# Last normalisation moved to ScalarE, limit copies moved to ScalarE, similarities ahead of the up projection

## What is computed

```python
q = jnp.einsum('bnd,de->bne', x, w_q)
q = (q - mean) * jax.lax.rsqrt(var + BN_EPS) * bn_gamma + bn_beta
sim = jnp.einsum('pbnhd,hkpd->pbnhk', q, keys)
sx, ix = jax.lax.top_k(sim[0], TOPK)
sy, iy = jax.lax.top_k(sim[1], TOPK)
all_scores = (sx[..., :, None] + sy[..., None, :]).reshape(b, n, H, TOPK * TOPK)
scores, pk = jax.lax.top_k(all_scores, TOPK)
h = jnp.einsum('bnd,bnhkd->bnhk', x, wd)
h = jax.nn.softmax(scores, axis=-1) * gelu_new(h)
out = jnp.einsum('bnhk,bnhkd->bnd', h, wu)
...
x = _layernorm(x + out)
```

## Time and profile before

| | us |
|---|---|
| median of 3 runs | 690.45 |
| lowest, highest | 686.77, 692.17 |
| the profiled execution, whole | 690.42 |
| its span | 688.1 |
| busy in the span: PE, DVE, ACT, POOL | 536.6, 559.7, 356.8, 442.5 |

### The profile page before, as it was taken

How to read it: one execution, slowest core, us unless ns; L and a number is a source line. 1 busy time by engine, 2 the same in 40 slices (tenths; PEclk the granted TensorE clock), 3 DMA queues, 4 the chain that set the end, 5 groups by cost and what they waited for, 6 DMA issues and landing times.

```text
span 688.1 us, 42215 instructions
## 1 busy us (share of the span) xinstructions
PE 536.6 (78%) x17863; PEld 455.5 (66%) x17863; DVE 559.7 (81%) x1837; ACT 356.8 (52%) x557; POOL 442.5 (64%) x615
## 2 busy tenths in 40 slices
PE   0475999999996899965667868778778778778765
PEld 0364888888885676855366757667667667667655
DVE  6544799899895678865698989999999999999962
ACT  4334577777774477751435445455445445445350
POOL 7533465655642344442387887898888898888870
PEclk9978899999999999986589999999999999999996
DMA  6786575654534010000032231322332331331320
GB/s 215 221 265 185 151 235 167 215 173 156 179 97 170 16 32 17 16 1 8 9 71 54 68 72 46 70 69 53 69 72 50 72 72 46 75 70 46 71 65 19
DMA packets 44934, 64.60 MB, mean 94 GB/s; under 512 B 5456, under 2 KB 37072, under 8 KB 42320
## 3 DMA queue, kind: packets, MB, share of 16 engines
q1 hardware_dynamic: 44880, 63.84, 33.1%
HBM read 36.29 MB, written 8.65 MB: 65 GB/s over the span
## 4 chain that ended last, share of the span: by engine, by line
PE 47%; DVE 31%; issue 14%; POOL 4%; ACT 1%; DMA 1%; DVEq 1%; SPq 0%; POOLq 0%; ACTq 0%
PE ps L743 9%; DVE top L1339 6%; PE ps L931 6%; PE ps L758 5%; PE ps L723 5%; PE ps L804 5%; DVE prod L1394 4%; PE ps L817 4%; DVE wq_sb L1370 4%; PE ps L733 3%; PE ps L910 3%; DVE best L1350 3%; DVE r_x L1379 3%; DVE hid L1385 2%; PE ps L769 2%
## 5 line engine op out<-in xcount | busy, mean ns | idle before, releaser
L931 PE MATMUL ps<-up_sb,prod 128*128 128x128 f32 x512 | 80.8, 320 | 48.5 <-DVE prod L1394 47.9
L931 PEld LDWEIGHTS ps<-up_sb,prod 128*128 128x128 f32 x512 | 74.4, 228 | 54.9 <-DVE prod L1394 54.4
L952 ACT ACTIVATE arena<-ps 128x512 f32<-128x512 f32 x128 | 70.2, 595 | 63.0 <-PE ps L743 62.9
L910 PE MATMUL ps<-arena,hid 128*32 128x32 f32 x8192 | 82.0, 200 | 23.9 <-issue 20.1
L910 PEld LDWEIGHTS ps<-arena,hid 128*32 128x32 f32 x8192 | 77.0, 112 | 29.3 <-issue 21.5
L658 POOL TENSOR_TENSOR wq_sb<-wq_sb,tile_rows 128x1024 f32<-128x1024 f32 x32 | 76.2, 2380 | 8.4 <-POOL tile_rows L654 7.2
L1072 ACT ACTIVATE out_tile<-ps,shift,rstd 128x128 f32<-128x128 f32 x32 | 14.6, 457 | 123.5 <-POOL shift L682 123.5
L1126 DVE TENSOR_REDUCE row_max<-ps 128x8 f32<-128x768 f32 x64 | 61.0, 952 | 19.8 <-PE ps L733 19.8
L743 PE MATMUL ps<-ident,arena 128*128 128x128 f32 x512 | 72.3, 288 | 1.1 <-issue 1.1
L919 PEld LDWEIGHTS ps<-xT,downT_sb 128*128 128x128 f32 x512 | 64.6, 198 | 11.9 <-issue 11.0
L1129 DVE TENSOR_TENSOR arena<-ps,row_max 128x768 f32<-128x768 f32 x64 | 61.3, 957 | 5.1 <-DVE row_max L1126 0.2
(11 more groups left out here) (157 smaller groups left out, 1299.0 us busy)
## 6 DMA issues: line engine op xcount, KB each, us to landing
arena<-r_x SPq DMA_DIRECT2D x128, 128.0 KB, 2.4
early<-terms SPq DMA_DIRECT2D x8, 720.0 KB
xT<-terms SPq DMA_DIRECT2D x8, 720.0 KB
hid<-terms SPq DMA_DIRECT2D x8, 720.0 KB
prod<-terms SPq DMA_DIRECT2D x8, 720.0 KB
x_pair<-in_x_wrapped SPq DMA_DIRECT2D x16, 256.0 KB, 2.6
x<-in_x SPq DMA_DIRECT2D x8, 256.0 KB, 2.8
xT_tile<-xT SPq DMA_DIRECT2D x32, 64.0 KB, 1.9
```

The source lines that it names most:

```text
L910: mm = nc.tensor.matmul(slots[32 * g:32 * g + 32, k, c], leftT[p][:, r // 2, r % 2, :], blocks_of[p][:, :, r // 2, r % 2, GROUP * g:GROUP ...
L931: mm = nc.tensor.matmul(ps[:, 6 + p, 0:P], pairs[:, c // 2, c % 2], up_sb[:, c, :], start=False, stop=(c == EC - 1))
L952: return nc.scalar.activation(out_ap, in_ap, ACT.Copy)
```

## The change

Four parts. (1) The last normalisation: DVE's bn_stats, bn_aggr and addition go; ACT takes minus the mean by a scaled Copy with an accumulated output (last_mean), the sum of squares by Square with the bias minus the mean (last_square), the variance plus epsilon (last_variance), and after POOL's power also the shift. POOL keeps the power alone (last_power), now of tile t - 3 and between the scaling of the exponentials and that of the right masks. (2) The two copies of limits go from POOL to ACT (set_limits); POOL's next tops and its thresholds wait for limits_set. (3) On PE the similarities of tile t + 2 stand ahead of the up projection of tile t - 1. (4) rel_exp is laid out with the eight heads of a key side by side: ACT writes with a step of 8 elements, POOL reads with a step of 1.

```diff
...
         limits = two("limits", [P, PK_HEADS, 10])
-        rel_exp = [tile_rows[:, 2560 + 512 * p:3072 + 512 * p].rearrange("p (a k) -> p a k", a=PH) for p in range(2)]
+        rel_exp = [tile_rows[:, 2560 + 512 * p:3072 + 512 * p].rearrange("p (a k h) -> p a k h", a=2, h=PK_HEADS) for p in range(2)]
...
                 pool.wait_ge(top_done, t + 1)
+                need(pool, limits_set, t)
                 hold(pool)
...
                 xs, ys = top_rel[:, 0:PK_HEADS, :], top_rel[:, PK_HEADS:PH, :]
-                nc.gpsimd.tensor_copy(limits[p][:, :, 2:5:2].rearrange("p h a -> p a h"),
-                                      top_rel[:, :, 1].rearrange("p (a h) -> p a h", a=2))
-                nc.gpsimd.tensor_copy(limits[p][:, :, 7:10:2], stretch(top_rel[:, 0:PK_HEADS, 1:2], 2))
                 nc.gpsimd.tensor_tensor(cand[:, :, 0:16].rearrange("p h (a b) -> p h a b", a=2),
...
                 pool.wait_ge(best_done, t + 1)
+                pool.wait_ge(limits_set, t + 1)
                 hold(pool)
...
-            def scale_right(t, p):
+            def scale_exps(t, p):
...
                 hold(pool)
-                ey = rel_exp[p][:, PK_HEADS:PH, :]
-                nc.gpsimd.tensor_tensor(ey, ey, bcast(rz[p][:], 2, KEYS), ALU.mult).then_inc(scaled, 1)
+                ey = rel_exp[p][:, 1]
+                nc.gpsimd.tensor_tensor(ey, ey, bcast(rz[p][:], 1, KEYS), ALU.mult).then_inc(scaled, 1)
+            def scale_right(t, p):
                 pool.wait_ge(scaled, t + 1)
...
                 hold(pool)
-                nc.gpsimd.tensor_tensor(right[p], right[p], bcast(ey.rearrange("p h j -> p j h"), 3, TERMS), ALU.mult
+                nc.gpsimd.tensor_tensor(right[p], right[p], bcast(rel_exp[p][:, 1], 3, TERMS), ALU.mult
                                         ).then_inc(right_ready, 1)
...
                 hold(pool)
-                ex = rel_exp[p][:, 0:PK_HEADS, :].rearrange("p h i -> p i h")
+                ex = rel_exp[p][:, 0]
                 nc.gpsimd.tensor_tensor(left[p][:, :, :, 0:TERMS - 1], left[p][:, :, :, 0:TERMS - 1],
...
-            def last_scale(t):
-
+            def last_power(t):
                 pool.wait_ge(d_var, t + 1)
-                hold(pool)
-                nc.gpsimd.tensor_tensor(rstd4[:], var4[:], minus_half[:, 0:1], ALU.pow).then_inc(rstd_step, 1)
-                pool.wait_ge(rstd_step, t + 1)
-                hold(pool)
-                nc.gpsimd.tensor_scalar(shift4[:], mom4[:, 0:1], rstd4[:], -1.0, ALU.mult, ALU.mult).then_inc(d_rstd, 1)
+                need(pool, out_ready, t)
+                hold(pool)
+                nc.gpsimd.tensor_tensor(rstd4[:], var4[:], minus_half[:, 0:1], ALU.pow).then_inc(d_rstd, 1)
...
                     t, o = 2 * i + p, 1 - p
+                    if have(t):
+                        scale_exps(t, p)
+                    if have(t - 3):
+                        last_power(t - 3)
                     if have(t):
...
                         scale_left(t, p)
-                    if have(t - 2):
-                        last_scale(t - 2)
             over_tiles(pool, d_pool)
+            last_power(NT - 1)
...
                     t, o = 2 * i + p, 1 - p
+                    if have(t + 2):
+                        similarities(t + 2, p, i + 1)
                     if have(t - 1):
                         up_projection(t - 1, o)
-                    if have(t + 2):
-                        similarities(t + 2, p, i + 1)
                     if have(t + 1):
...
                 need(a, left_ready, t - 1)
-                nc.scalar.activation(rel_exp[p].rearrange("p a k -> p (a k)"), ps[:, p, :], ACT.Exp
+                nc.scalar.activation(rel_exp[p].rearrange("p a k h -> p a h k"),
+                                     ps[:, p, :].rearrange("p (a h k) -> p a h k", a=2, h=PK_HEADS), ACT.Exp
                                      ).then_inc(relexp_done, 1)
+            def set_limits(t, p):
+                a.wait_ge(top_step, t + 1)
+                need(a, masked, 2 * (t - 1))
+                copy(limits[p][:, :, 2:5:2].rearrange("p h a -> p a h"), top_rel[:, :, 1].rearrange("p (a h) -> p a h", a=2))
+                copy(limits[p][:, :, 7:10:2], stretch(top_rel[:, 0:PK_HEADS, 1:2], 2)).then_inc(limits_set, 1)
+            def last_mean(t, p):
+                a.wait_ge(up_done, t + 1)
+                nc.scalar.activation(scratch[:], ps[:, 6 + p, 0:P], ACT.Copy, scale=-1.0 / P, accum_out=minus_mean4[:]
+                                     ).then_inc(d_mean, 1)
+            def last_square(t, p):
+                a.wait_ge(d_mean, t + 1)
+                nc.scalar.activation(scratch[:], ps[:, 6 + p, 0:P], ACT.Square, bias=minus_mean4[:], accum_out=square4[:]
+                                     ).then_inc(d_square, 1)
+            def last_variance(t):
+                a.wait_ge(d_square, t + 1)
+                nc.scalar.activation(var4[:], square4[:], ACT.Identity, bias=eps_col[:], scale=1.0 / P).then_inc(d_var, 1)
             def last_norm(t, p, i):
                 a.wait_ge(d_rstd, t + 1)
+                nc.scalar.activation(shift4[:], minus_mean4[:], ACT.Copy, scale=rstd4[:]).then_inc(d_shift, 1)
+                a.wait_ge(d_shift, t + 1)
                 need(a, stored[p], 16 * i)
...
+            a.wait_ge(eps_ready, 1)
             a.wait_ge(w_sim_done, 1)
...
                         rel_exps(t + 1, o)
+                        set_limits(t + 1, o)
+                    if have(t - 2):
+                        last_mean(t - 2, p)
+                    if have(t + 1):
                         best_exps(t + 1, o)
                     if have(t - 2):
+                        last_square(t - 2, p)
+                        last_variance(t - 2)
                         last_norm(t - 2, p, i - 1)
...
-            def last_moments(t, p):
-                v.wait_ge(up_done, t + 1)
-                V.bn_stats(stats4[:], ps[:, 6 + p, 0:P]).then_inc(d_step, 1)
-                v.wait_ge(d_step, 2 * t + 1)
-                need(v, out_ready, t)
-                hold(v)
-                V.bn_aggr(mom4[:], stats4[:]).then_inc(d_step, 1)
-                v.wait_ge(d_step, 2 * t + 2)
-                V.tensor_scalar(var4[:], mom4[:, 1:2], EPS, None, ALU.add).then_inc(d_var, 1)
-
             v.wait_ge(x3_kept, NQ)
...
                         top_keys(t + 1, o)
-                    if have(t - 2):
-                        last_moments(t - 2, p)
                     if have(t):
```

More of the change, by code:

```diff
@@ L216, in attention_and_product_keys @@
         out_tile = two("out_tile", [P, P])
-        stats4 = sb("stats4", [P, 6])
-        mom4 = sb("mom4", [P, 2])
+        scratch = sb("scratch", [P, P])
+        eps_col = sb("eps_col", [P, 1])
+        minus_mean4 = sb("minus_mean4", [P, 1])
+        square4 = sb("square4", [P, 1])
         var4 = sb("var4", [P, 1])
@@ L317, in attention_and_product_keys @@
         up_done = sem("up_done")
-        d_step = sem("d_step")
+        eps_ready = sem("eps_ready")
+        limits_set = sem("limits_set")
+        d_mean = sem("d_mean")
+        d_square = sem("d_square")
         d_var = sem("d_var")
-        rstd_step = sem("rstd_step")
         d_rstd = sem("d_rstd")
+        d_shift = sem("d_shift")
         out_ready = sem("out_ready")
@@ L496, in _ @@
             nc.gpsimd.memset(ones[:], 1.0)
+            nc.gpsimd.memset(eps_col[:], EPS).then_inc(eps_ready, 1)
             nc.gpsimd.memset(zeros[:], 0.0)
@@ L1311, in split_constants @@
                 cols = slice(Q_SPLIT[part].start * KEYS, Q_SPLIT[part].stop * KEYS)
-                c_rest = rel_exp[0].rearrange("p a k -> p (a k)")
+                c_rest = rel_exp[0].rearrange("p a k h -> p (a k h)")
                 v.wait_ge(c_row_done, part + 1)
```

## The result

The changed kernel takes 670.03 us (median of 4 runs, 669.26 to 671.22), the kernel before beside it 690.11 (4 runs, 686.77 to 692.17): a ratio of 0.971, 95% interval 0.967 to 0.975. The prediction was 668.9 (659 to 683). The profiled execution took 669.26 with a span of 667.4, 20.7 less than before.

The account below looks back on a forecast made before the run. VectorE bounds the kernel before; after the change a GpSimd-ScalarE chain of waits lies beside VectorE's floor. Gains of 20.2 (usual tiles) and 2.0 (slow tiles), less 0.7 (end), make 21.5: 690.4 - 21.5 = 668.9 us, range 659 to 683.

Parts of the forecast that it names:

- Removed from DVE: Last normalisation's moments leave VectorE: 0.82 us a tile, lowering its floor from 10.04 to 9.22 us.
- The new ring of waits: Closed chain of waits between GpSimd and ScalarE, one turn per tile: 9.25 us, tile taken as 9.32; gain 20.2 us.
- I take 0.07: Extra time for ScalarE's exponentials written 32 bytes apart: 0.07 us a tile, with 1.05 as the far end.
- I take 0.53: Saving at GpSimd's left scaling from reading the eight heads side by side: 0.53 us, bounds 0 to 0.53.
- Normalisation to exponentials: ScalarE's stretch from the start of the last normalisation to the start of the next exponentials: 4.42 us of the chain.
- Rival C: ScalarE's spread write costs 2 ns each, a turn of 10.23 us: 694.4 us, no change that can be told; chance 0.07.
- rival B: GpSimd reads the spread rows no faster, a turn of 9.78 us: 681.8 us; chance 0.13.
- The slow tiles: Eight tiles with TensorE at its lower clock: of 1.0 us each, 0.75 returns as VectorE's wait; gain 2.0 us.
- The end: Last tile's normalisation at the kernel's end, covered by nothing: 2.0 us on ScalarE, 0.7 us lost.
- What would show it: Trace signs: tiles 9.2 to 9.4, left scaling about 1.47, right about 1.9, exponentials 0.6 to 0.7, waits at the edges.
- Rival A: Waits between GpSimd and ScalarE do not bound, VectorE alone does: 661.3 us; chance 0.17.
- D: Spread rows cost rather than save, at ScalarE's exponentials, a turn of 10.76 us: 709.3 us, slower; chance 0.05.

Follow-up runs that it names:

- the limits first: Changed kernel with ScalarE's limit copies ahead of its exponentials instead of behind them: 664.49 us, ratio 0.964; again on another chip 664.54 us, ratio 0.958.
- the fillers: Four needless 128x128 products ahead of TensorE's wait for the gate, added to the changed kernel with similarities back behind the up projection: 677.22 us, ratio 0.981.

## Why the prediction was right

The path was right: DVE's work falls, and the new ring, which had no slack, sets the tile. Two sizes were wrong in opposite directions.

**Removed from DVE: right.** The floor is 9.29 by the run with the limits first, 9.22 predicted.

**The new ring of waits: right as a mechanism, 0.25 short as a size, and the tile with it 0.18.** Three runs show it: shortened, the tiles fall to DVE's floor; lengthened by 0.49, they grow by 0.42; the same work beside it costs nothing. The ring was predicted at 9.25 and the tile at 9.32; both are 9.50 in the mean (turns of 9.57 and 9.43). The mis-sized terms are those of the spread rows. The exponentials: "I take 0.07" was the near end; from their start to the limit copies they take 0.90 against 0.67. The left scaling: "I take 0.53", it gave 0.40. L659, counted at its old 0.62, takes 0.69: the edit changed its operands too, and the prediction left that out. "Normalisation to exponentials" gave 0.10 back. Rival C had the mechanism, 2 ns a write of the 512; it measures (1114 - 598) / 512 = 1.0 ns, half of that; and of the saving that rival B denied, 0.40 of 0.53 is there. Neither decided, since the costs and the saving come out nearly even. The argument against B set 1.67 ns an element, without the fixed part of an instruction, beside 2.6 with it; like with like it is 1.67 against 2.36, which still speaks against B.

The Trainium skill (Advanced Engine Details and Errata, Memory Cachelines) spoke against the spread write; the trace agrees, at 1.0 ns an element where every one lies on another line. The rule of the Trainium skill on the read side (GPSIMD Engine Reference, Performance pitfalls for Q7 kernels) would have given 0.7 us at the left scaling, an estimate from its figures; measured were 0.40, in the right direction.

**The slow tiles: the term that failed.** It took the low clock itself as given. From the tenth tile's first MAX8 to the last tile's the kernel before takes 652.85 - 426.65 = 226.20 and the changed one 631.54 - 422.28 = 209.26, 16.9 less in 22 tiles. Usual tiles give 22 x (10.05 - 9.50) = 12.1 of it, where 15.8 were predicted, and the five slow tiles the remaining 4.8, where five times 0.25, 1.3, were predicted: 3.7 lost at one term and 3.5 gained at the other. "So of the 1.0 us that such a tile costs before, 0.75 comes back as a wait of DVE for the limits" has no case of its own in the changed kernel: from 425 us to the last first MAX8 no up projection runs at the lower clock. The one late low-clock tile, with its wait of 0.89, shows the way from a late down projection to DVE, but the delay came from PE's pause and the similarities. So the size of 0.75 stays untested.

**The end: right.** After the last first MAX8 the kernel before takes 688.1 - 652.85 = 35.3 and the changed one 35.9: 0.6 lost, 0.7 predicted.

**What would show it: mostly right.** Tiles of 9.2 to 9.4 were to be seen, and 9.50 are; the exponentials of over 1 us that were to speak for C are there too, and the signs named for the ring are there: the wait at the edges, in every second tile, and the thresholds released by the limit copies. The two scalings came out longer than named, 1.60 for about 1.47 and 2.02 for about 1.9. Rival A falls by the wait at the edges, B by the 1595 ns, C and D by the sum.

**Open.** What decides the clock within PE's idle time isn't settled. The wait ahead of the up projection doesn't by itself: with the limits on GpSimd it lasts up to 1.48, 27.6 us in all from 425 to 625, and the clock stays at 1.00, against 26.6 us in all with the similarities back and a clock of 0.90 to 0.97; and in the kernel with the normalisation alone up projections at the low clock follow waits of 1.21 to 1.37, and those behind its waits of 1.74 run at the full one. Why the first pass through the loop stops PE for "issue" wasn't tried (2.40 us in the kernel before and in the changed one alike), nor whether the fillers lengthen these pauses.

## What to carry to other kernels

When work leaves the bounding engine, add up the closed chain of waits that the new handovers make, start to start, and look for what stands in it without need: here one swap of two calls on an engine with idle time was worth another 5.5 us. A layout change has a price at everyone who touches the data, the writer and the in-place step between included; list all of them before taking the reader's gain. And a low-clock tile is not a fixed cost to be carried over: here fewer gaps on TensorE took it away, and faster tiles with the old order brought more of them.

## Not expected of the hardware

ACT's write of 512 elements 32 bytes apart took 1114 ns against 598 for a dense one, with the same input; the next instruction on ACT started 0.90 after its start in place of 0.50. Each accumulated output of ACT appears as an instruction of its own (ACTIVATION_READ_ACCUMULATOR, 195 to 203 ns), half of it beside the ACTIVATE ahead of it. And filling TensorE's idle time with products that nobody reads kept its granted clock at 1.00 from 425 to 625 us, where 0.90 to 0.97 were granted without.
